# Attention operands of the first item copied by chunk, and its values moved between engines, in a two-layer transformer kernel

## The chip, the cores and the metric

The kernel runs on one core of one Trainium2 chip. The metric is the device time of one execution, in microseconds (us). Engines are named as in the profile: PE is TensorE, DVE is VectorE, ACT is ScalarE, POOL is GpSimd, SP is SyncE, whose queue issues the DMA transfers here.

## The reference

Two post-norm transformer layers over x of shape (2, 1024, 256), with 16 heads of 16. In layer 0 four heads share one group of keys and values:

```python
q = (x @ Wq + bq).reshape(B, T, 16, 16).transpose(0, 2, 1, 3)
k = (x @ Wk + bk).reshape(B, T, 4, 16).transpose(0, 2, 1, 3)
v = (x @ Wv + bv).reshape(B, T, 4, 16).transpose(0, 2, 1, 3)
k, v = jnp.repeat(k, 4, axis=1), jnp.repeat(v, 4, axis=1)
q_hat, k_hat = q / (norm(q) + EPS), k / (norm(k) + EPS)
scores = einsum(rope(q_hat * alpha * 4), rope(k_hat)) / 4      # causal
y = softmax(scores) @ v @ Wo + bo
x = layernorm(x + y)
x = layernorm(x + mxfp4(x) @ mxfp4(W).T + bias)                # layer 0's FFN
```

Layer 1 is an attention with 16 key heads (no normalisation of q and k), and a mixture of 8 experts, top 2, with a shared expert.

## The kernel before

**Tiling.** The 2048 tokens are 4 chunks of 512 (`NC`, `CH`). The kernel goes through a head (projections, rotation and lengths of layer 0's q and k, and its v), the attention of layer 0, a middle (layer 0's FFN and layer 1's projections), the attention of layer 1, and a tail with the experts. Every engine has one program, written out by hand in the order of the code; semaphores join them. An engine's instructions start in that order, so one that waits holds up all behind it.

**The head** (`head`) has 12 units `u`, three tiles for each chunk. For each unit: TensorE projects, DVE multiplies with the rotation tables (`turned`, L814), TensorE adds the rotated part, ACT keeps the result in a slot of `ops_mem` (`rot(u)`, `keep`, L742) and squares it; TensorE sums the squares and DVE turns them into factors per chunk (`factors`). TensorE transposes them (L689), ACT copies them (`keep_factors`, L763), TensorE spreads them over the rows (`spread_factors`, L699), DVE multiplies (`normalised`, L823). The product is split into three bf16 parts, high, middle and low: ACT casts the high part (`keep_hi`, L752), DVE subtracts it (`less_hi`, L830), ACT casts the middle part (`keep_mid`, L756), and GpSimd subtracts for the low part (L801), which counts in `s_parts[0]`. The values of the four chunks come from TensorE (L651); DVE adds the bias and writes them to `vres` (`values`, L833, L839). Those of chunks 2 and 3 stand in DVE's program between `less_hi(7)` and `less_hi(8)` (L901, L902).

**The attention** (`attention`, both layers) has 8 items, `NI`: 2 batches by 4 groups of 4 heads. Item `i` has two passes `c` of 512 queries over 12 steps `s` of 128 keys. TensorE makes scores (`scores`, L1238) into one of three pairs of PSUM banks, ACT takes the exponential (L1319), GpSimd masks the diagonal steps (L1335), TensorE multiplies with the values (`values_product`, L1255) into bank 6, two steps later. After each pass DVE copies bank 6 to `raw` (`take`, L1155), and `normalise` (L1157) transposes, inverts, transposes and multiplies into `yT` (L1162 to L1167). The first product of a pass waits until the take of the pass before is done (`s_taken`). DVE sets out the values of an item in `vstat` (L1149).

**Operands** (`Operands`). Scores contract over 99 rows: six combinations of parts by 16, and three rows for a shift. `stack(sp, i)` (L953) copies them from `parts_mem` to `qT` and `kT`, both in `ops_mem`, with two buffers `buf = i % 2`: 18 transfers in layer 0 and two more for the three rows (zeros on the q side, ones on the k side) for the first two items. In layer 1 there are 26. SP's order in each attention is: stack of item 0 once six units of parts are there (two chunks, batch 0), stack of item 1 once all parts are there, `no_shift` (L983), then the stacks of items 2 to 7:

```python
                ops.stack(sp, 0)
                sp.wait_ge(s_parts[layer], TILES[layer] * NC)
                ops.stack(sp, 1)
                ops.no_shift(sp)
                sp.wait_ge(ops.s_zero, 16 * GH)
```

`no_shift` fills `shiftT` with zeros in four transfers of three rows each. `shiftT` lies in `yT`, so DVE waits for them (`ops.s_zero`, L1186) after item 0's first take and ahead of its first `normalise`. From item 2 on a stack also waits for the scores of the item before last.

**The flag block** (`maxima`). Before each attention DVE and TensorE load a flag from memory and jump over a long block (`dve.If`, `pe.If`) that is only needed if scores could overflow; with these inputs it is jumped. In DVE's program the values of item 0 come behind that jump (`values(dve, 0)` in `attention`). TensorE's program behind it waits for free banks (`banks_free`, L912) and for item 0's stack (`ops.there(pe, 0)`), and makes the scores of the first two steps; then it waits for the values and makes those of the third.

**Where the buffers lie.** `ops_mem` columns 0 to 2047 and 4096 to 6143 are buffer 0 of `qT` and `kT`; the other halves are buffer 1. The kept tiles of units 0 to 5 lie in buffer 0, those of units 6 to 11 in buffer 1.

Of the kernel before, what the change touches and what calls it, by code (L numbers as in the profile page):

```python
# [17 lines left out]
T = 1024  # L18
# [50 lines left out]
def build(nc, a, out):  # L69
    ctx = ExitStack()  # L70
    with ctx:
# [506 lines left out]
        s_v, s_bo = sem("s_v1"), sem("s_bo")  # L578
        YN_COUNT, YN_HALF = 18, 11
# [13 lines left out]
        def head():  # L593
# [32 lines left out]
            def rot(u):  # L626

                b, j = u // (NU // 2), u % (NU // 2)
                o = 2048 * b + 512 * j if j < 4 else 4096 + 2048 * b + 512 * (j - 4)
                return ops_mem[:, o:o + 512]  # L630
# [174 lines left out]
            def _(dve):  # L805
# [95 lines left out]
                values(2)  # L901
                values(3)  # L902
# [9 lines left out]
            def banks_free(pe):  # L912

                pe.wait_ge(s_a_read, len(ORDER))
# [23 lines left out]
        class Operands:  # L938


            def __init__(self, layer):
# [3 lines left out]
                self.s_shifted = sem(f"s_shifted{layer}")  # L945
                self.s_zero, self.s_decided = sem(f"s_zero{layer}"), sem(f"s_decided{layer}")
                self.s_scores = sem(f"s_scores{layer}")

            def count(self, i):

                return 2 * NSLOT + (NSLOT if self.layer == 0 else 2 * NSLOT) + (2 if i < 2 else GH)

            def stack(self, sp, i):  # L953
# [20 lines left out]
                if i < 2:  # L974
                    sp.dma_start(qT[ROWS:KDIM, buf, :, :], a["zeros"][:, 0:GH * T].rearrange("r (h n) -> r h n", h=GH)
                                 ).then_inc(s, 16)
                    sp.dma_start(kT[ROWS:KDIM, buf, :, :], a["ones"].rearrange("r (h n) -> r h n", h=GH)
                                 ).then_inc(s, 16)
# [10 lines left out]
            def shift(self, dve, i):  # L989

                dve.wait_ge(self.s_stacked[i], 16 * self.count(i))
                for h in range(GH):
                    last = nc.vector.tensor_copy(qT[ROWS:KDIM, i, h, :], shiftT[32 * h:32 * h + 3, i, :])
                last.then_inc(self.s_shifted, 1)

# [122 lines left out]
        def attention(layer, ops, first, banks_free, buffer_free, gates=None, finish=None, ahead=None):  # L1118
            kh = KEYS_OF[layer]
            s_vstat = sem(f"s_vstat{layer}")  # L1120
# [14 lines left out]
            def _(sp):  # L1135
                buffer_free(sp)
                ops.stack(sp, 0)
# [8 lines left out]

            def values(dve, i):
                buf = i % 2
                nc.vector.tensor_copy(vstat[:, buf, :, 0:kh, HD * buf:HD * buf + HD],  # L1149
# [1077 lines left out]
```

## Time and profile before

| what | value |
|---|---|
| median of 3 runs | 809.42 us (808.75 to 810.59) |
| the profiled execution's own time | 807.32 us |
| its span | 805.6 us |
| TensorE busy | 728.9 us (90%) |
| DVE busy | 413.4 us (51%) |
| ACT busy | 394.9 us (49%) |
| GpSimd busy | 168.5 us (21%) |
| mean granted TensorE clock | 0.955 of full speed |

The profile is of one execution; its own time is 1.7 us over its span. A busy time says how long an engine had an instruction in it, and its share of the span is an average over parts of the kernel with different limits. The order of time gives, for each instruction, its start, its length and, in square brackets, how long its engine idled before it and what ended that; "issue" stands for an idle time that no event of the profile explains. An "x8" is a run of eight like instructions told as one line.

### The profile page before, as it was taken

To read this page: it belongs to the slowest core of one execution; us is meant where nothing else is said; L and a number is where in the kernel's file an instruction comes from. 1 tells how busy PE (TensorE), PEld (TensorE's weight loads), DVE (VectorE), ACT (ScalarE), POOL (GpSimd) and SP (SyncE) were. 2 spreads that over 40 slices of the span, in tenths; PEclk is the share of its full clock that TensorE was granted. 3 is DMA by queue.
4 is the path that set the end of the run, shared out by engine and by line. 5 is a ranking of instruction groups with operands and counts; after the bars stand their busy time and mean duration, and the time that the engine had idled before them with its cause. 6 is when DMAs were issued, how large, how long until landed. Compare 5 with 4: busy or idle time off the path is not lost.

```text
span 805.6 us, 10853 instructions
## 1 busy us (share of the span) xinstructions
PE 728.9 (90%) x3786; PEld 329.3 (41%) x3786; DVE 413.4 (51%) x998; ACT 394.9 (49%) x517; POOL 168.5 (21%) x185
## 2 busy tenths in 40 slices
PE   5998699999988867886999999989999999999996
PEld 1645222224322533442222222324466457448355
DVE  1578435334769798855043333365432842642524
ACT  1244688886877252543788888774121121130110
POOL 0012434443233132322133222331200200000000
PEclk9996599999999989879799999999999999999998
DMA  8401423332210000032444444470000000000000
GB/s 279 114 0 20 71 53 59 55 54 40 37 35 2 1 0 14 0 52 41 80 79 83 82 80 81 81 201 0 1 1 0 27 0 1 26 0 0 26 1 26
DMA packets 31602, 36.37 MB, mean 45 GB/s; under 512 B 7664, under 2 KB 19757, under 8 KB 31389
## 3 DMA queue, kind: packets, MB, share of 16 engines
q1 hardware_dynamic: 31541, 35.60, 21.8%
q8 instruction: 33, 0.54, 0.3%
q14 instruction: 28, 0.23, 0.1%
HBM read 12.74 MB, written 2.10 MB: 18 GB/s over the span
## 4 chain that ended last, share of the span: by engine, by line
PE 63%; DVE 15%; SPq 10%; ACT 5%; issue 4%; DMA 2%; POOL 0%; DVEq 0%; ACTq 0%; POOLq 0%
PE ps L1988 16%; PE ps L1255 12%; PE ps L1238 9%; PE ps L2012 9%; SPq L972 4%; SPq L965 4%; ACT probs L1319 3%; PE ps L1618 2%; PE ps L1605 2%; PE ps L398 2%; DVE stats L289 1%; PE ps L1632 1%; PE ps L643 1%; DVE raw L1155 1%; PE ps L1998 1%
## 5 line engine op out<-in xcount | busy, mean ns | idle before, releaser
L1319 ACT ACTIVATE probs<-ps 128x1024 f32<-128x1024 f32 (+1 forms) x320 | 276.0, 967 | 66.0 <-PE ps L1238 65.7
L1238 PE MATMUL ps<-ops_mem 99*128 99x512 bf16 (+3 forms) x768 | 164.0, 335 | 15.1 <-issue 5.5
L1255 PE MATMUL ps<-probs,vstat 128*32 128x512 f32 (+3 forms) x1536 | 166.1, 505 | 11.7 <-DVE raw L1155 7.4
L1988 PE MATMUL ps<-ops_mem,parts_mem 128*128 128x512 f32 x320 | 146.1, 602 | 1.2 <-DVE probs L2040 1.2
L1335 POOL TENSOR_SCALAR_AFFINE_SELECT probs<-probs 128x512 f32<-128x512 f32 x128 | 84.6, 661 | 225.3 <-ACT probs L1319 224.6
L1238 PEld LDWEIGHTS ps<-ops_mem 99*128 99x128 bf16 x768 | 57.6, 99 | 164.3 <-ACT probs L1319 87.9
L1155 DVE COPY raw<-ps 128x512 f32<-128x512 f32 x32 | 22.1, 691 | 140.8 <-PE ps L1255 140.6
L1934 ACT ACTIVATE ops_mem<-ps 128x512 f32<-128x512 f32 x40 | 23.9, 597 | 141.1 <-PE ps L1988 141.1
L1988 PEld LDWEIGHTS ps<-ops_mem,parts_mem 128*128 128x128 f32 x320 | 58.5, 190 | 67.8 <-issue 65.1
L2012 PE MATMUL ps<-parts_mem,probs 128*128 128x256 f32 x320 | 70.5, 380 | 0.0
L2012 PEld LDWEIGHTS ps<-parts_mem,probs 128*128 128x128 f32 x320 | 60.4, 190 | 8.3 <-issue 0.5
L1255 PEld LDWEIGHTS ps<-probs,vstat 128*32 128x32 f32 x1536 | 31.3, 108 | 73.9 <-issue 49.4
L2035 DVE TENSOR_TENSOR probs<-ops_mem,ps 128x512 f32<-128x512 f32 x40 | 27.5, 687 | 63.7 <-ACT ops_mem L1934 63.0
L1755 POOL TENSOR_TENSOR parts_mem<-probs,parts_mem 128x512 bf16<-128x512 f32 x16 | 22.0, 1387 | 68.3 <-ACT parts_mem L1725 68.3
L1162 DVE STREAM_TRANSPOSE den<-raw 128x512 f32<-128x512 f32 x32 | 22.7, 708 | 22.2 <-DMA yT<-in_zeros 21.5
L643 PE MATMUL ps<-yT,probs 128*128 128x512 f32 x48 | 27.2, 695 | 7.3 <-DMA yT<-in_xT 7.3
L1618 PE MATMUL ps<-ops_mem,w1qkv 128*128 128x512 f32 x64 | 30.9, 606 | 0.0
L744 ACT COPY ops_mem<-ps 128x512 f32<-128x512 f32 x12 | 7.0, 584 | 44.5 <-PE ps L667 44.5
L801 POOL TENSOR_TENSOR parts_mem<-parts_mem 128x512 bf16<-128x512 f32 x12 | 13.7, 1152 | 71.6 <-ACT parts_mem L756 71.5
L1167 DVE TENSOR_TENSOR yT<-raw,den 128x512 f32<-128x512 f32 x32 | 27.1, 848 | 1.1
L2040 DVE TENSOR_TENSOR probs<-probs,ps 128x512 f32<-128x512 f32 x32 | 22.0, 687 | 9.4 <-PE ps L1998 7.2
L1632 PE MATMUL ps<-probs,perm 128*128 128x512 f32 x32 | 21.9, 774 | 4.4 <-DVE probs L1784 4.4
(185 smaller groups left out, 720.8 us busy)
## 6 DMA issues: line engine op xcount, KB each, us to landing
ops_mem<-parts_mem SPq DMA_DIRECT2D x288, 64.0 KB
yT<-in_xT SPq DMA_DIRECT2D x4, 512.0 KB, 8.0
xres<-in_x SPq DMA_DIRECT2D x1, 2048.0 KB, 14.3
ops_mem<-parts_mem SPq DMA_DIRECT2D x48, 32.0 KB
out<-ops_mem SPq DMA_DIRECT2D x3, 512.0 KB, 3.0
rope<-in_rope SPq DMA_DIRECT2D x1, 1024.0 KB, 6.7
parts_mem<-in_wg SPq DMA_DIRECT2D x2, 512.0 KB, 5.9
parts_mem<-in_wu SPq DMA_DIRECT2D x2, 512.0 KB, 7.4
```

Source lines behind the costliest of these rows:

```text
L643: last = nc.tensor.matmul(ps[:, A + AT[m, n] % 2, :], w0qkv[:, kk, n * P:(n + 1) * P], xT0[:, kk, m * CH:(m + 1) * CH], start=kk == 0, sto ...
L965: sp.dma_start(qT[n * HD:n * HD + HD, buf, j::2, :], tq[32 * g + HD * j:32 * g + HD * j + HD, Q_PARTS[n], :, toks]).then_inc(s, 16)
L972: sp.dma_start(kT[n * HD:n * HD + HD, buf, j::2, :], tk[32 * g + HD * j:32 * g + HD * j + HD, K_PARTS[n], :, toks]).then_inc(s, 16)
L1155: nc.vector.tensor_copy(raw[:, :], ps[:, AV, :]).then_inc(s_taken, 1)
L1238: last = nc.tensor.matmul(ps[:, bank, o:o + CH - lo], kT[0:KDIM, buf, h if kh == GH else 0, kt * P:(kt + 1) * P], qT[0:KDIM, buf, h, c * C ...
L1255: last = nc.tensor.matmul(ps[32 * h:32 * h + 32, AV, lo:CH], vstat[:, i % 2, kt, h if kh == GH else 0, :], probs[:, s % PRING, h, 0:CH - l ...
L1319: nc.scalar.activation(o, banks, ACT.Exp, scale=score_scale).then_inc(s_exp, 1)
L1335: nc.gpsimd.affine_select(out=block_, in_=block_, compare_op=ALU.is_ge, fill=0.0, base=0, pattern=[[0, GH], [1, P]], channel_multiplier=-1 ...
L1618: last = nc.tensor.matmul(ps[:, A + n % 2, :], w1qkv[:, kk, n * P:(n + 1) * P], xT1[:, kk, :], start=kk == 0, stop=kk == 1)
L1632: nc.tensor.matmul(ps[:, R + u % 2, :], perm[:, :], u_sin[:, u % 2, :], start=False, stop=True).then_inc(s_rot, 1)
L1988: last = nc.tensor.matmul(ps[:, 4 + 2 * (e % 2) + m, :], w, xT[:, kk, :], start=kk == 0, stop=kk == 1)
L2012: last = nc.tensor.matmul(ps[:, t // 2, (t % 2) * C:(t % 2) * C + C], hT[:, e, t * P:(t + 1) * P], w, start=e == 0, stop=e == NE - 1)
```

## The change

It has five parts.

1. `rot(u)` uses eight slots in buffer 1 alone, in turn; from unit 8 on ACT waits for the product (`s_qn`) that frees the slot. Buffer 0 stays free.
2. Item 0's stack in layer 0 is `stack_first`: first the two transfers of zeros and ones, then chunk 0's 18 transfers when three low parts are written, then chunk 1's 18 when six are. The first 20 count in a new semaphore `s_early`, the others in the old one. TensorE waits for `s_early` before item 0's scores, and for the rest before step 4, the first of the second pass.
3. The values of item 0 are set out by DVE ahead of the flag block, in both layers (`first_values`); in layer 1 they wait for the values of two chunks instead of four.
4. The values of chunks 2 and 3 are copied from PSUM by ACT without the bias (`keep_values`), behind `keep_hi(7)` and `keep_hi(8)`.
5. GpSimd adds the bias to them in eight instructions, behind item 0's fourth mask; DVE waits for that before it sets out the values of item 4.

```diff
             def rot(u):
-                b, j = u // (NU // 2), u % (NU // 2)
-                o = 2048 * b + 512 * j if j < 4 else 4096 + 2048 * b + 512 * (j - 4)
+                j = u % 8
+                o = 2048 + 512 * j if j < 4 else 6144 + 512 * (j - 4)
                 return ops_mem[:, o:o + 512]
...
                 def keep(u):
                     act.wait_ge(s_rot, u + 1)
+                    if u >= 8:
+                        act.wait_ge(s_qn, u - 7)
...
+                def keep_values(m):
+                    act.wait_ge(s_a, AT[m, NTL] + 1)
+                    nc.scalar.copy(vres[:, NG:2 * NG, m % 2 * CT:(m % 2 + 1) * CT, 0:HD].rearrange("p g t d -> p t g d"),
+                                   ps[:, A + AT[m, NTL] % 2, 0:CT * 64].rearrange("p (t g d) -> p t g d", t=CT, g=NG)
+                                   ).then_inc(s_v0, 1)
...
                 keep_hi(7)
+                keep_values(2)
                 keep_mid(6)
                 keep_hi(8)
+                keep_values(3)
                 keep_factors(3)
...
                 less_hi(7)
-                values(2)
-                values(3)
                 less_hi(8)
...
-                pe.wait_ge(s_a_read, len(ORDER))
+                pe.wait_ge(s_a_read, len(ORDER) - 2)
+                pe.wait_ge(s_v0, 2)
...
+            def stack_first(self, sp):
+                s = self.s_stacked[0]
+                self.rows(sp, 0, self.s_early)
+                for m in range(2):
+                    toks = slice(m * CH, (m + 1) * CH)
+                    sp.wait_ge(s_parts[0], TILES[0] * (m + 1))
+                    for n in range(NSLOT):
+                        for j in range(2):
+                            sp.dma_start(qT[n * HD:n * HD + HD, 0, j::2, toks],
+                                         tq[HD * j:HD * j + HD, Q_PARTS[n], :, toks]
+                                         ).then_inc((self.s_early, s)[m], 16)
+                        sp.dma_start(kT[n * HD:n * HD + HD, 0, 0, toks], tk0[0:HD, K_PARTS[n], 0, toks]
+                                     ).then_inc((self.s_early, s)[m], 16)
...
-                ops.stack(sp, 0)
+                if layer == 0:
+                    ops.stack_first(sp)
+                else:
+                    ops.stack(sp, 0)
...
-                if layer == 1:
-                    dve.wait_ge(s_v, 2 * NC)
-                values(dve, 0)
...
-                ops.there(pe, 0)
+                if layer == 0:
+                    ops.early(pe)
+                else:
+                    ops.there(pe, 0)
...
                     for s in range(LAG, NS):
+                        if layer == 0 and i == 0 and s == 4:
+                            ops.there(pe, 0)
...
                         if layer == 0 and d == 3:
+                            if i == 0:
+                                pool.wait_ge(s_v0, 2)
+                                loaded(pool, "head")
+                                for t in range(TPB):
+                                    v = vres[:, NG:2 * NG, t, 0:HD]
+                                    last = nc.gpsimd.tensor_tensor(v, v, b_v[:, :].rearrange("p (g n) -> p g n", g=NG),
+                                                                   ALU.add)
+                                last.then_inc(s_v0, 1)
...
+        def first_values(layer):
+            @on("vector")
+            def _(dve):
+                if layer == 1:
+                    dve.wait_ge(s_v, NC)
+                values(dve, layer, 0)
+
+        first_values(0)
         maxima(0, ops[0])
...
+        first_values(1)
         maxima(1, ops[1])
```

## Rows read from the trace of the kernel before

**Rows 1.** The page: busy us (share of the span) x instructions.

```profile
PE 728.9 (90%) x3786; PEld 329.3 (41%) x3786; DVE 413.4 (51%) x998; ACT 394.9 (49%) x517; POOL 168.5 (21%) x185
```

**Rows 2.** Order of time, head: start us, us, engine, instruction [idle before].

```profile
62.06 1.15 POOL L801 TENSOR_TENSOR parts_mem<-parts_mem 128x512 bf16<-128x512 f32 x1 [2.94 <-ACT parts_mem L756]
...
83.30 1.14 DVE L839 TENSOR_TENSOR vres<-ps,b_v 128x64 f32<-128x64 f32 x8
...
83.31 0.58 ACT L763 COPY probs<-ps 60x512 bf16<-60x512 bf16 x1
...
84.95 1.29 DVE L823 TENSOR_TENSOR ps<-ps,ops_mem 128x512 f32<-128x512 f32 x2
...
87.71 3.46 POOL L801 TENSOR_TENSOR parts_mem<-parts_mem 128x512 bf16<-128x512 f32 x3 [0.80 <-ACT parts_mem L756]
```

**Rows 3.** The same view by engine, beginning of item 0 of layer 0.

```profile
82.25 0.63 PE L689 MATMUL ps<-identb,probs 128*60 128x128 bf16 x4 [0.47 <-DVE probs L870]
...
89.83 3.15 PE L1238 MATMUL ps<-ops_mem 99*128 99x512 bf16 x8 [4.07 <-DMA ops_mem<-in_ones]
...
90.94 3.35 ACT L1319 ACTIVATE probs<-ps 128x1024 f32<-128x1024 f32 x4 [1.36 <-PE ps L1238]
...
93.33 0.44 DVE L1149 COPY vstat<-vres 128x128 f32<-128x128 f32 x1 [4.39 <-issue]
```

**Rows 4.** The same view, the SP queue's issues.

```profile
74.83 1.44 SPq L965 DMA_DIRECT2D ops_mem<-parts_mem  x2
...
91.20 1.26 SPq L965 DMA_DIRECT2D ops_mem<-parts_mem  x2
...
103.57 3.14 SPq L986 DMA_DIRECT2D yT<-in_zeros  x4
```

**Rows 5.** The same view, end of item 0 and beginning of item 1.

```profile
112.79 0.71 DVE L1162 STREAM_TRANSPOSE den<-raw 128x512 f32<-128x512 f32 x1 [10.68 <-DMA yT<-in_zeros]
...
114.06 0.43 PE L1255 MATMUL ps<-probs,vstat 128*32 128x128 f32 x8
...
114.57 0.64 POOL L1335 TENSOR_SCALAR_AFFINE_SELECT probs<-probs 128x512 f32<-128x512 f32 x1 [2.03 <-ACT probs L1319]
...
114.58 1.17 DVE L1167 TENSOR_TENSOR yT<-raw,den 128x512 f32<-128x512 f32 x1
...
115.78 0.69 DVE L1155 COPY raw<-ps 128x512 f32<-128x512 f32 x1
...
116.62 1.06 PE L1255 MATMUL ps<-probs,vstat 128*32 128x512 f32 x8 [1.47 <-POOL probs L1335]
```

**Rows 6.** The same view, layer 1: the flag, first scores, item 1's first product.

```profile
378.93 0.14 DVE L1071 TENSOR_SCALAR flag<-guard 1x1 int32<-1x1 f32 x1
...
383.26 2.50 PE L1238 MATMUL ps<-ops_mem 99*128 99x512 bf16 x6 [5.18 <-issue]
...
409.83 1.06 PE L1255 MATMUL ps<-probs,vstat 128*32 128x512 f32 x8 [1.47 <-POOL probs L1335]
```

**Rows 7.** Groups by shape, ACT: xcount | busy us, mean ns | idle before.

```profile
L477 ACT ACTIVATE small<-small 128x32 f32<-128x32 f32 x4 | 0.9, 229 | 15.3 <-DVE small L495 15.3
```

**Rows 8.** The order of time, GpSimd's fifth mask and a later product of DVE.

```profile
108.42 0.63 POOL L1335 TENSOR_SCALAR_AFFINE_SELECT probs<-probs 128x512 f32<-128x512 f32 x1 [9.66 <-ACT probs L1319]
...
118.28 0.69 DVE L1167 TENSOR_TENSOR yT<-raw,den 128x512 f32<-128x512 f32 x1
```

**Rows 9.** TensorE after stalls; two stretches: us, busy (x), granted clock, DMA, GB/s.

```profile
229.31 1.07 PE L1255 MATMUL ps<-probs,vstat 128*32 128x512 f32 x8 [2.28 <-DVE raw L1155]
...
263.14 1.09 PE L1594 MATMUL ps<-ident,xres 128*128 128x128 f32 x8 [2.90 <-DVE raw L1155]
...
291.14 0.58 PE L1625 MATMUL ps<-none 1*128 1x512 bf16 x1 [5.29 <-DVE probs L1796]
...
265.00:269.00 4.00, 3.67 (x10) 0.57 0.01 4
...
291.00:298.00 7.00, 5.98 (x17) 0.65 0.00 0
```

More of the change, by code:

```diff
@@ L578, in build @@
         s_v, s_bo = sem("s_v1"), sem("s_bo")
+        s_v0 = sem("s_v0")
         YN_COUNT, YN_HALF = 18, 11
@@ L949, in count, with rows @@
             def count(self, i):
+                if self.layer == 0 and i == 0:
+                    return 3 * NSLOT
                 return 2 * NSLOT + (NSLOT if self.layer == 0 else 2 * NSLOT) + (2 if i < 2 else GH)
+            def stack_first(self, sp):
[11 more added lines that the diff above has]
+                                     ).then_inc((self.s_early, s)[m], 16)
+            def rows(self, sp, buf, s):
+                sp.dma_start(qT[ROWS:KDIM, buf, :, :], a["zeros"][:, 0:GH * T].rearrange("r (h n) -> r h n", h=GH)
+                             ).then_inc(s, 16)
+                sp.dma_start(kT[ROWS:KDIM, buf, :, :], a["ones"].rearrange("r (h n) -> r h n", h=GH)
+                             ).then_inc(s, 16)
             def stack(self, sp, i):
@@ L974, in stack @@
                 if i < 2:
[L975 to L978, printed above, removed]
+                    self.rows(sp, buf, s)
                 else:
@@ L991, in shift @@
                 dve.wait_ge(self.s_stacked[i], 16 * self.count(i))
+                if i == 0 and self.layer == 0:
+                    self.early(dve)
                 for h in range(GH):
@@ L994, in shift, with early @@
                 last.then_inc(self.s_shifted, 1)
+            def early(self, eng):
+                eng.wait_ge(self.s_early, 16 * (3 * NSLOT + 2))
             def there(self, pe, i):
@@ L1119, in attention @@
             kh = KEYS_OF[layer]
-            s_vstat = sem(f"s_vstat{layer}")
             s_scores = ops.s_scores
@@ L1145, in _ @@
                     ops.stack(sp, i)
-            def values(dve, i):
-                buf = i % 2
-                nc.vector.tensor_copy(vstat[:, buf, :, 0:kh, HD * buf:HD * buf + HD],
-                                      vres[:, i, :, 0:kh * HD].rearrange("p t (n d) -> p t n d", d=HD)
-                                      ).then_inc(s_vstat, 1)
             def take(dve, i, c):
@@ L1182, in _ @@
                     if i + 1 < NI:
-                        values(dve, i + 1)
+                        values(dve, layer, i + 1)
                     if i == 0:
@@ L1265, in _ @@
                 next(free)
-                ops.there(pe, 0)
+                if layer == 0:
+                    ops.early(pe)
+                else:
+                    ops.there(pe, 0)
                 scores(0, 0)
@@ L1271, in _ @@
                     more = i + 1 < NI
-                    pe.wait_ge(s_vstat, i + 1)
+                    pe.wait_ge(s_vstat[layer], i + 1)
                     for s in range(LAG, NS):
+                        if layer == 0 and i == 0 and s == 4:
+                            ops.there(pe, 0)
                         scores(i, s)
@@ L1327, in _ @@
                         pool.wait_ge(s_y, NI)
-                        pool.wait_ge(s_vstat, NI // 2)
+                        pool.wait_ge(s_vstat[layer], NI // 2)
                         for g in range(NG // 2):
@@ L1347, in _ @@
                                 pool.wait_ge(s_y, NI)
-                                pool.wait_ge(s_vstat, NI // 2)
+                                pool.wait_ge(s_vstat[layer], NI // 2)
                                 ahead.stage(pool, 0)
@@ L2095, in build, with values @@
         ops = [Operands(layer) for layer in range(2)]
+        s_vstat = [sem(f"s_vstat{layer}") for layer in range(2)]
+        def values(dve, layer, i):
+            buf, kh = i % 2, KEYS_OF[layer]
+            if i == NI // 2:
+                dve.wait_ge(*((s_v0, 3) if layer == 0 else (s_v, 2 * NC)))
+            nc.vector.tensor_copy(vstat[:, buf, :, 0:kh, HD * buf:HD * buf + HD],
+                                  vres[:, i, :, 0:kh * HD].rearrange("p t (n d) -> p t n d", d=HD)
+                                  ).then_inc(s_vstat[layer], 1)
+        def first_values(layer):
[5 more added lines that the diff above has]
+        first_values(0)
         maxima(0, ops[0])
```

1 line of the change is left out of this document (added).

## The prediction

> **What bounds the kernel now.** I read the page first, to see which engine the time hangs on. TensorE is busy nine tenths of the span [rows 1]. So a change pays only where it shortens a stretch in which TensorE stands idle, and only if nothing later in that stretch waits for something else.
>
> Next I read the order of time around the join of layer 0's head and its attention, as that is where the edits lie. Five things are to be seen there.
>
> First, how the head ends [rows 2]. DVE does its eight value adds (L839) from 83.30 to 84.44, between two subtractions; ACT copies the last factors at 83.31, TensorE spreads them, DVE multiplies at 84.95. From there the work is a strict relay of DVE and ACT to GpSimd's last three subtractions, which end at 87.71 + 3.46 = 91.17.
>
> Second, how item 0 begins [rows 3]. TensorE is idle from 85.76 to 89.83, until the ones of buffer 0 have landed. Its first two groups of scores end at 89.83 + 3.15 = 92.98, and the third stands behind the values, which DVE sets out from 93.33 to 93.77, after its flag. DVE's own way past the flag block costs it 4.39 us.
>
> Third, the SP queue [rows 4]. The first stack is issued from 74.83, when the sixth low part is written. The second starts at 91.20, 0.03 us after GpSimd's last subtraction, and its 20 transfers take SP to 103.57: 0.62 us each. Behind it come the four zero transfers, to 106.71.
>
> Fourth, **the wait that ends last at item 0's end** [rows 5]. After item 0's first take DVE idles 10.68 us for those zeros. From 112.79 it is one run of work: transpose, reciprocal, transpose, product, then the second take of `raw`, 115.78 to 116.47. TensorE had ended item 0's last product at 114.06 + 0.43 = 114.49 and item 1's third scores at 115.15; it idles 1.47 us to 116.62, when item 1's first product may overwrite the accumulator. The row names GpSimd, but the mask of that product was done at 115.21 and the take ended at 116.47: it is the take. Without the zeros it could have begun at about 114.5.
>
> Fifth, layer 1 has the same pattern: TensorE idles 1.47 us before item 1's first product at 409.83 [rows 6].
>
> **The change part by part.**
>
> *Operands by chunk, into a buffer kept free.* The ones and zeros rows go out long before, the first chunk's 18 transfers when three low parts are written (GpSimd's third ends at 62.06 + 1.15 = 63.21 [rows 2]) and the second chunk's 18 behind them. At 0.62 to 0.64 us each, the half-size ones taken like whole ones, that is 63.2 to 74.7 and then, as the sixth part is there at 74.80, to 86.4. SP issues 18 transfers more than before, and is still free 4.8 us before 91.2; only if each took over (91.2 - 63.2) / 36 = 0.78 us would the second stack slip. The eight-slot ring for the rotated tiles adds a wait of ACT on products that DVE finished several tiles earlier: nothing.
>
> TensorE's start is then no longer the DMA but its own way past the flag block. The trace doesn't show that alone. Its upper bound is the 4.07 us gap of before. In layer 1 it is 383.26 - 379.07 = 4.19 with the flag's load in it [rows 6]; in layer 0 that load fits into the 0.47 us before the factors' transposes at 82.25 [rows 3], so I take 3.7: start at 89.46 for 89.83, 0.37 earlier. The lower bound is near nothing (start at 85.8). The Trainium skill (Runtime: NRT & Kernel Launch, Instruction fetch mechanics) says that a taken branch to a page not yet fetched stops the engine for a fetch; Advanced Engine Details and Errata (Control Flow Timing) has about 108 ns for a compare and branch, by which TensorE would start some 3.9 us earlier. The 4.39 us on DVE and the 4.19 on TensorE speak for the first.
>
> *First values ahead of the flag.* The third scores then wait for two exponentials only. Four of those take 3.35 us from 90.94; two, from 0.37 earlier, end near 90.57 + 1.8 = 92.4. So the third scores start at 92.4 where they stood behind 93.77: **1.4 us earlier**. Bounds: 1.0 with no earlier start (two end at 92.8); 2.3 with an immediate one, as ACT is busy with the head's parts to 90.94 - 1.36 = 89.58 [rows 3]. So item 0 ends 1.0 to 2.3 us earlier. In layer 1 the copy now stands ahead of the flag's arithmetic: 0.43 us later there at most, covered by the 1.47 us that TensorE idles before 409.83; without that cover it would be a loss of 0.4.
>
> *Last values by ACT.* DVE is freed of 1.14 us of work between 83.30 and 84.35. ACT gains two copies of 128x256. No row is just that: 0.23 us for 32 columns [rows 7] and 0.58 for 512 [rows 2] bound it, and by a straight line it is 0.39. The second copy stands ahead of the last factors: 83.31 becomes about 83.70, the spread 84.3, done at 84.9. DVE was busy to 84.95 before and now is free at 84.2, so its product starts at 84.9 again. The two edits cancel: bounds -0.2 to +0.2 us on 91.17, for copies of 0.23 to 0.58. GpSimd's eight bias adds of 128x64 come after item 0's fourth mask; by 1.15 us for 512 columns [rows 2] each is about 0.15, by 1.15 at worst 9.2 in all, and GpSimd idles 9.66 us before its fifth mask at 108.42 [rows 8]: hidden. DVE's wait for them is at item 4.
>
> **The sum.** The 1.4 us is won ahead of item 0 and lost at its end. The zeros are behind the second stack, which is bound to 91.17, and that moves by 0 +- 0.2. So they land at 112.8 and TensorE goes on at 116.6; its idle stretch grows from 1.47 to 1.47 + 1.4 = 2.9 us. What is left is the product at 114.58, which took 1.17 us beside a mask of GpSimd and 0.69 without one [rows 5, 8]; the masks shift by 1.4, and I count half of the 0.48: -0.24. The profiled run is 807.32 (span 805.6), 2.1 under the median 809.42; the difference of -0.24 put on the median gives **809.2**.
>
> **Rivals.**
>
> *The clock falls in the longer stall (slower).* TensorE idled 2.28 us before 229.31 and kept its speed: eight products in 1.07 us, as the 1.06 at 409.83 [rows 6, 9]. After idling 5.29 us before 291.14 it ran at a lower granted clock, and also after 2.90 us before 263.14 [rows 9]. The new stall, 2.5 to 3.8 us, lies between. At half clock matmuls take up to twice as long. The granted clock was 0.57 over the 4 us from 265, a mixture of its levels 1 (2.4 GHz) and 0.5 (1.2 GHz): (1 - 0.57) / 0.5 x 4 = 3.4 us stood at half, which costs half of that, 1.7; after 291 it was 0.65 over 7 us, 4.9 us, with 2.4 as the most. That puts the time at 809.2 + 1.7 = 810.9, up to 811.6. It decides if the stall comes near those that lost the clock. The Trainium skill (TensorE: Matmul & The Clock Gate, HAM oscillation) warns of just this, the idle engine being put back to half rate; by its word the result would be that 810.9. Chance 0.20.
>
> *The start's gain comes through (faster).* If the zeros don't bind, or land sooner, item 1's first product starts one take (0.69) after item 0's last product, at about 114.5 - 1.4 + 0.8 = 113.9, 2.7 us earlier: 806.7, with bounds 805.8 and 807.1 from the bounds of 1.4. Against it stands the 10.68 us row [rows 5], and that the edits leave the zeros where they are in SP's order. Chance 0.15.
>
> *The head gets shorter.* If ACT's copies hide entirely, part of the 1.14 us reaches 91.17 and all behind it: 808.3 to 809. Chance 0.10.
>
> *It does not do what it says.* If the flag block takes the whole gap, TensorE starts at 89.83 as before; only 1.0 us moves, and is swallowed too: 809.4. Chance 0.10.
>
> **How the numbers follow.** My forecast has 0.42, and 0.03 is left for things unseen. No change within 0.2% (1.6 us, about what a measurement of this kernel can tell from no change) means 807.8 to 811.0: the forecast, the shorter head, the inactive change and half of the clock case, 0.42 + 0.10 + 0.10 + 0.10 = 0.72; I shade it to 0.66, as TensorE's start is poorly bounded on both sides, which gives faster 0.17 and slower 0.17. The range takes in most of both rivals: 806.6 to 811.5. The forecast's own range is 808.8 to 809.8.
>
> **What would show it.** Right: the first scores near 89.5, the third near 92.4; GpSimd's last subtraction at 91.2; zeros landed at 112.8; DVE's second take at 115.3 to 115.8; TensorE idle near 3 us before item 1's first product. The first branch cost is wrong if the first scores start before 88. The forecast is wrong if that product starts before 115.5, or if the granted clock is under 1 between 113 and 125. Layer 1 should stand at the same distances as before.

## The result, and the profile after

The changed kernel is slower. Its median is 813.92 us (810.08 to 817.5, 22 runs) where the kernel before, timed beside it, has 810.49 (806.99 to 816.41, 22 runs); the ratio is 1.0035 with a 95% interval of 1.002 to 1.005, which is 1.6 to 4 us. The profiled execution has a span of 811.0 us. I forecast 809.2, no change, with 806.6 to 811.5 as the range; on the kernel before's first median, 809.42, the ratio gives 812.3, above the range.

The profile of the kernel before is one of its fastest executions: 807.32 us where its median is 810.49. Its granted clock stands at 1.00 from 98 to 264 us and from 392 to 800 us, where the changed kernel's has 0.96 and 0.99. So the two profiles lie further apart than the medians, and the reading has to go place by place.

Four lines of the page: the span, the busy times, TensorE's granted clock in 40 slices, and the shares of the chain that ended last by engine.

```profile
span 811.0 us, 10879 instructions
...
PE 732.4 (90%) x3786; PEld 330.4 (41%) x3786; DVE 411.1 (51%) x990; ACT 395.5 (49%) x519; POOL 170.6 (21%) x193
...
PEclk9996689999989889899799999999999999999998
...
PE 61%; DVE 16%; SPq 11%; issue 4%; ACT 3%; DMA 3%; POOL 1%; DVEq 0%; ACTq 0%; POOLq 0%
```

TensorE is busy 3.5 us longer with the same 3786 matmuls [rows 1], so it did the same work more slowly. The order of time at the end of the head and the beginning of item 0 (start us, us, engine, instruction, [idle before]):

```profile
63.00 1.43 SPq L981 DMA_DIRECT2D ops_mem<-parts_mem  x2
...
82.85 0.38 ACT L766 COPY vres<-ps 128x256 f32<-128x256 f32 x1
...
84.40 1.30 DVE L837 TENSOR_TENSOR ps<-ps,ops_mem 128x512 f32<-128x512 f32 x2 [0.72 <-PE ps L701]
...
87.17 3.48 POOL L815 TENSOR_TENSOR parts_mem<-parts_mem 128x512 bf16<-128x512 f32 x3 [0.61 <-ACT parts_mem L761]
...
87.93 4.20 PE L1274 MATMUL ps<-ops_mem 99*128 99x512 bf16 x12 [2.72 <-issue]
...
88.31 0.22 DVE L2154 COPY vstat<-vres 128x128 f32<-128x128 f32 x1
...
89.04 4.26 ACT L1361 ACTIVATE probs<-ps 128x1024 f32<-128x1024 f32 x5
...
90.68 1.25 SPq L1006 DMA_DIRECT2D ops_mem<-parts_mem  x2
...
92.07 1.65 PE L1291 MATMUL ps<-probs,vstat 128*32 128x512 f32 x8
...
103.46 3.14 SPq L1024 DMA_DIRECT2D yT<-in_zeros  x4
```

Here nearly everything came as forecast. The head ran about half a microsecond early as a whole in this execution. Against that, DVE's multiplication at 84.40 stands where it stood before, ACT's copy takes 0.38 us (I took 0.39), and the second stack and the zeros start at 90.68 and 103.46 (91.20 and 103.57 in [rows 4]). But TensorE's first scores start at 87.93, with 2.72 us for the way past the flag block where I took 3.7 (2.5 to 3.1 in all nine profiles with operands copied by chunk), and ACT gets through its first five exponentials without a gap. Item 0's first product with the values starts at 92.07; in the kernel before it is this line, 2.7 us later:

```profile
94.79 1.94 PE L1255 MATMUL ps<-probs,vstat 128*32 128x512 f32 x8
```

The same view, end of item 0 and beginning of item 1, with item 1's first and second takes as the last lines:

```profile
110.54 0.43 PE L1291 MATMUL ps<-probs,vstat 128*32 128x128 f32 x8
...
112.63 0.71 DVE L1201 STREAM_TRANSPOSE den<-raw 128x512 f32<-128x512 f32 x1 [14.04 <-DMA yT<-in_zeros]
...
114.41 0.69 DVE L1206 TENSOR_TENSOR yT<-raw,den 128x512 f32<-128x512 f32 x1
...
115.14 0.69 DVE L1194 COPY raw<-ps 128x512 f32<-128x512 f32 x1
...
115.97 1.94 PE L1291 MATMUL ps<-probs,vstat 128*32 128x512 f32 x8 [4.35 <-DVE raw L1194]
...
123.26 0.69 DVE L1194 COPY raw<-ps 128x512 f32<-128x512 f32 x1 [4.93 <-PE ps L1291]
...
136.50 0.69 DVE L1194 COPY raw<-ps 128x512 f32<-128x512 f32 x1 [4.21 <-PE ps L1291]
```

Item 0's last product ends at 110.97, 3.5 us earlier than in [rows 5]. The zeros land at 112.63, as before, and DVE has waited 14.04 us for them instead of 10.68. DVE's product is down to 0.69 us. The take is at 115.14, TensorE's product at 115.97: 0.65 us earlier than before, after a stall of 4.35 us. And now eight products take 1.94 us instead of 1.06.

TensorE's busy time and clock by stretches of the changed kernel (stretch in us, length, busy and instructions, granted clock, DMA share, GB/s):

```profile
86.00:92.00 6.00, 4.02 (x12) 0.50 0.09 19
...
92.00:98.00 6.00, 6.00 (x47) 0.89 0.48 83
...
98.00:112.00 14.00, 13.42 (x100) 1.00 0.30 54
...
112.00:124.00 12.00, 7.88 (x47) 0.72 0.43 73
...
113.80:120.60 6.80, 4.63 (x22) 0.50 0.50 86
```

The same stretches of the kernel before, where they differ most:

```profile
92.00:98.00 6.00, 5.15 (x28) 0.51 0.49 85
...
112.00:124.00 12.00, 10.32 (x85) 1.00 0.40 69
```

Two things happened to the clock. It rose sooner (0.89 against 0.51 in the stretch from 92), which made item 0 shorter than I had reckoned and the stall longer. And it fell in the stall: 0.72 over the 12 us from 112, that is (1 - 0.72) / 0.5 x 12 = 6.7 us at 1.2 GHz, from 113.8 to 120.6. TensorE had 4.63 us of work in it; at full clock that would be half, 2.3 us less.

From here on I read one distance in every kernel: from item 0's second take to item 1's second take. In the kernel before it is 135.03 - 115.78 = 19.25, here 136.50 - 115.14 = 21.36. The line of the kernel before that [rows 5] doesn't hold:

```profile
135.03 0.69 DVE L1155 COPY raw<-ps 128x512 f32<-128x512 f32 x1 [4.21 <-PE ps L1255]
```

So the stall cost 2.11 us behind it; less the 0.64 us that the take was early, every take of the changed kernel up to item 6's first is 1.47 us later than in the kernel before. Behind that, this execution lost 2.7 us more at item 6 and 1.6 at the last item of layer 1, in two stalls of 2.29 and 1.74 us. Stalls of the same length stand in the kernel before, where the clock held in them; runs below show that it falls there in some executions with and without the change. Whether the change makes those falls more frequent isn't shown.

In layer 1 the copy that now stands ahead of the flag took 1.24 us, not the 0.43 that I had taken, while GpSimd was subtracting, and TensorE's first scores there come after 5.94 us of idleness instead of 5.18:

```profile
381.15 1.24 DVE L2154 COPY vstat<-vres 128x512 f32<-128x512 f32 x1
...
387.24 2.19 PE L1274 MATMUL ps<-ops_mem 99*128 99x512 bf16 x5 [5.94 <-issue]
```

### The profile page after: what moved, and what is told of

Same layout as the page of the kernel before. It is cut to its first block, busy times and chain, and to the rows that moved or that the text cites. A ratio compares the mean times of both kernels' runs of the same rounds, so it can differ in the third digit from the quotient of the medians.

```text
span 811.0 us, 10879 instructions
## 1 busy us (share of the span) xinstructions
PE 732.4 (90%) x3786; PEld 330.4 (41%) x3786; DVE 411.1 (51%) x990; ACT 395.5 (49%) x519; POOL 170.6 (21%) x193
## 4 chain that ended last, share of the span: by engine, by line
PE 61%; DVE 16%; SPq 11%; issue 4%; ACT 3%; DMA 3%; POOL 1%; DVEq 0%; ACTq 0%; POOLq 0%
PE ps L2039 16%; PE ps L1291 11%; PE ps L2063 9%; PE ps L1274 8%; SPq L1006 5%; SPq L1013 4%; PE ps L1669 2%; PE ps L1656 2%; PE ps L398 2%; DMA yT<-in_zeros 2%; ACT probs L1361 2%; DVE stats L289 2%; DVE raw L1194 1%; PE ps L645 1%; PE ps L669 1%
## 5 line engine op out<-in xcount | busy, mean ns | idle before, releaser
L1291 PE MATMUL ps<-probs,vstat 128*32 128x512 f32 (+3 forms) x1536 | 168.8, 512 | 14.9 <-DVE raw L1194 11.9
L1274 PE MATMUL ps<-ops_mem 99*128 99x512 bf16 (+3 forms) x768 | 165.9, 338 | 14.3 <-issue 9.5
L645 PE MATMUL ps<-yT,probs 128*128 128x512 f32 x48 | 25.3, 651 | 7.2 <-DMA yT<-in_xT 7.2
L1669 PE MATMUL ps<-ops_mem,w1qkv 128*128 128x512 f32 x64 | 30.9, 605 | 0.0
L1683 PE MATMUL ps<-probs,perm 128*128 128x512 f32 x32 | 20.2, 717 | 4.4 <-DVE probs L1835 4.4
```

What stands on the lines that cost most here:

```text
L645: last = nc.tensor.matmul(ps[:, A + AT[m, n] % 2, :], w0qkv[:, kk, n * P:(n + 1) * P], xT0[:, kk, m * CH:(m + 1) * CH], start=kk == 0, sto ...
L1274: last = nc.tensor.matmul(ps[:, bank, o:o + CH - lo], kT[0:KDIM, buf, h if kh == GH else 0, kt * P:(kt + 1) * P], qT[0:KDIM, buf, h, c * C ...
L1291: last = nc.tensor.matmul(ps[32 * h:32 * h + 32, AV, lo:CH], vstat[:, i % 2, kt, h if kh == GH else 0, :], probs[:, s % PRING, h, 0:CH - l ...
L1669: last = nc.tensor.matmul(ps[:, A + n % 2, :], w1qkv[:, kk, n * P:(n + 1) * P], xT1[:, kk, :], start=kk == 0, stop=kk == 1)
```

## The experiments

**Theory 1**: the gain ahead of item 0 is lost at the zeros, and the stall that takes its place costs TensorE its clock. **Theory 2**, in one form or another: the loss comes from the other edits (ACT's copies, GpSimd's adds, 18 more transfers, layer 1's copy), or from the length of the stall alone. Twelve kernels test them. Each was timed in five rounds against the kernel before; ratios are against that, with 95% intervals. Each has one profile. "The distance" is that between the two takes above.

### The zeros in SP's gap

```diff
+                if layer == 0:
+                    banks_free.mem_free(sp)
+                    ops.no_shift(sp)
                 sp.wait_ge(s_parts[layer], TILES[layer] * NC)
                 ops.stack(sp, 1)
-                ops.no_shift(sp)
+                if layer == 1:
+                    ops.no_shift(sp)
```

`mem_free`, whose definition is left out here, has SP wait until TensorE has made the head's last projection and its last sum of squares, so that the head is done with `yT`.

On the changed kernel:

> The changed kernel, with the four zero transfers of layer 0 issued between the first item's last copies and the second stack, in the gap in which SP stands idle (about 87.5 to 90.7 us). Theory 1 (the gain ahead of item 0 is lost at the zeros, and TensorE's clock falls in the stall there): the zeros land by 97, no stall of over 0.5 us before item 1's first product, which starts at 111.5 to 113 for 115.97; the granted clock stays 1.0 from 112 to 125; the time is 4 to 7 us under the kernel before, ratio 0.991 to 0.995. Theory 2 (the loss comes from the other edits: ACT's copies, GpSimd's adds, more transfers, the copy ahead of layer 1's flag): that product starts earlier, but no more than 2 us of it is left at the end of layer 0, and the ratio stays at 0.999 or over.

Measured: ratio 0.9961 (0.9937 to 0.9985), median 806.74. Its order of time, SP's zeros, DVE's work after item 0, and TensorE's first product of item 1:

```profile
87.51 3.15 SPq L1029 DMA_DIRECT2D yT<-in_zeros  x4
...
98.58 0.69 DVE L1203 COPY raw<-ps 128x512 f32<-128x512 f32 x1 [9.69 <-PE ps L1300]
...
99.37 0.71 DVE L1210 STREAM_TRANSPOSE den<-raw 128x512 f32<-128x512 f32 x1
...
111.91 0.69 DVE L1203 COPY raw<-ps 128x512 f32<-128x512 f32 x1 [10.06 <-PE ps L1300]
...
112.75 1.07 PE L1300 MATMUL ps<-probs,vstat 128*32 128x512 f32 x8 [0.31 <-DVE raw L1203]
```

The zeros were there when DVE wanted them (its transpose follows the first take at once), the stall is 0.31 us, the product starts at 112.75, and the distance of the takes is 19.25 again. All takes up to the end of layer 0 are 3.87 us earlier than before. By the ratio the kernel is 3.2 us (1.2 to 5.1) faster than the one before, with all the other edits in place. That speaks against Theory 2's first form, and it is less than the 4 to 7 us that I expected: in this profile the last take of layer 1 is only 1.48 us early, and the clock fell once near 538 and once near 562 us, where it had held in the profile of the kernel before.

On the kernel before:

> The kernel before with the same move of the zeros alone. Theory 1: the stall of 1.47 us shrinks to 0.3, the product starts at 115.4 for 116.62, ratio 0.998 to 0.999; so the change is worth 3 to 4 us once the zeros are out of the way. Theory 2: the same 1.2 us here, but the changed kernel with the zeros moved is no faster than this one.

Measured: the stall shrank to 0.31 us and the distance from item 0's first take to its second from 14.50 to 13.33 us, the expected 1.2. The ratio, 1.0017 (0.9992 to 1.0042) for 0.998 to 0.999 expected, doesn't show it; in its profile the clock fell at item 6's stall. So the time alone leaves the 1.2 us unproven. But it answers Theory 2: of the two kernels with the zeros moved, timed side by side, the changed one has 806.74 against 810.63, so the change is worth 3.9 us once the zeros are out of the way (3 to 4 expected).

### The stall filled with work

```diff
                         scores(i, s)
+                        if layer == 0 and i == 1 and s == LAG:
+                            for _ in range(16):
+                                nc.tensor.matmul(ps[:, 7, :], kT[0:KDIM, 1, 0, 0:P], qT[0:KDIM, 1, 0, 0:CH],
+                                                 start=True, stop=True)
                         values_product(i, s - LAG)
```

> The changed kernel with 16 matmuls of 128x512 more, whose result nobody reads, in front of item 1's first product, so that TensorE has work in the stall. Nothing else is moved. Theory 1: the product starts at 115.9 to 116.2 as in the changed kernel, but the granted clock stays 1.0 until 125 and the next take of DVE comes at 121.2 to 121.6 for 123.26 (1.5 to 2.1 us earlier); ratio 0.999 to 1.001. Theory 2: the take stays within 0.5 us of 123.26 or the ratio stays at 1.003.

Measured: ratio 0.9979 (0.9957 to 1.0001), median 807.58. Order of time:

```profile
111.67 3.62 PE L1319 MATMUL ps<-ops_mem 99*128 99x512 bf16 x16
...
114.93 0.69 DVE L1194 COPY raw<-ps 128x512 f32<-128x512 f32 x1
...
115.77 1.06 PE L1291 MATMUL ps<-probs,vstat 128*32 128x512 f32 x8 [0.48 <-DVE raw L1194]
...
120.95 0.69 DVE L1194 COPY raw<-ps 128x512 f32<-128x512 f32 x1 [2.82 <-PE ps L1291]
...
134.18 0.69 DVE L1194 COPY raw<-ps 128x512 f32<-128x512 f32 x1 [4.21 <-PE ps L1291]
```

and the stretch from 112 to 124, with its granted clock:

```profile
112.00:124.00 12.00, 11.37 (x78) 1.00 0.43 73
```

Sixteen matmuls whose result nobody reads make the changed kernel faster; the interval lies wholly under its own, 1.002 to 1.005. The product starts at 115.77, nearly as without them, the clock stays at 1.00, the distance of the takes is 19.25, and the next take came at 120.95 (123.26 - 120.95 = 2.31 us sooner, for 2.11 + the 0.20 by which the product starts earlier). This is the strongest evidence for Theory 1: nothing about the waits is changed, only what TensorE does during one. The take came a little earlier and the ratio lower than expected (121.2 to 121.6; 0.999 to 1.001). Between the middles of the two ratios lie 4.5 us, twice what the takes show; the other half has no place in these profiles that I can name.

### The stall lengthened in the kernel before

```diff
                         dve.wait_ge(ops.s_zero, 16 * GH)
+                        if layer == 0:
+                            dve.wait_ge(s_taken, 1)
+                            for n in range(4):
+                                nc.vector.transpose(den[:, :], raw[:, :]).then_inc(s_delay, 1)
+                                dve.wait_ge(s_delay, n + 1)
```

> The kernel before with four more transposes of DVE (0.71 us each, into a buffer that is written again at once) after the zeros' wait, which lengthens the stall before item 1's first product from 1.47 to about 4.4 us and changes nothing else. Theory 1: the product starts 2.9 to 3.0 us later, at 119.6, the clock falls to 0.5 behind it, and the next take is 4.4 to 5.2 us later than 121.79; ratio 1.0055 to 1.0065. Theory 2 (a stall costs its own length): the next take is 2.9 to 3.1 us later, ratio 1.0035 to 1.004.

```profile
118.24 1.94 PE L1261 MATMUL ps<-probs,vstat 128*32 128x512 f32 x8 [3.79 <-DVE raw L1156]
```

and its stretch:

```profile
112.00:124.00 12.00, 8.14 (x61) 0.86 0.48 82
```

Measured: from item 0's first take to its second 16.82 us for 14.50, and the distance of the takes 138.07 - 117.40 = 20.67 for 19.25. So the kernel before gets the same disease from a longer stall alone: 2.3 us for the delay (the stall is 3.79 us, not 4.4) and 1.4 for the clock. The next take itself came at 124.87, 3.08 us behind 121.79. By the letter that is Theory 2's forecast of 2.9 to 3.1; but this execution was 0.70 us early at item 0's first take, and from there the next take is 3.78 us later, which a delay of 2.3 us alone doesn't give. The ratio is 1.0091 (1.0062 to 1.0121), 5 to 10 us, more than both: in its profile the clock also fell at item 1's stall of layer 1, which was 2.36 us long. The direction is shown, the size in the time was under-expected.

### Parts of the change undone

The first values of layer 0 behind the flag again:

```diff
-        first_values(0)
         maxima(0, ops[0])
+        first_values(0)
```

> The changed kernel with layer 0's first values behind the flag again, as in the kernel before. Theory 1 (the stall before item 1's first product is as long as the start of item 0 is early): the third group of scores waits for the values, near 92.7 for 91.3, item 0 ends about 1.5 us later than in the changed kernel, the stall is 2.5 to 3.3 us for 4.35; the product starts at 115.9 to 116.1 all the same. The clock may fall or not; if it does the next take is at 123.0 to 123.4, if not at 121 to 121.3. Theory 2 (the early values themselves cost): the next take is at 121.8 or earlier with the clock fallen.

```profile
91.90 1.03 PE L1274 MATMUL ps<-ops_mem 99*128 99x256 bf16 x4 [0.89 <-DVE vstat L2154]
...
115.84 1.06 PE L1291 MATMUL ps<-probs,vstat 128*32 128x512 f32 x8 [1.83 <-DVE raw L1194]
```

Its stretches from 112 and from 226:

```profile
112.00:124.00 12.00, 9.96 (x83) 1.00 0.43 74
...
226.00:238.00 12.00, 9.71 (x46) 0.72 0.10 19
```

Measured: ratio 0.9999 (0.9974 to 1.0024). The third scores wait for the values (0.89 us), the clock rises later (0.50 from 92 to 98, for 0.89), the stall is 1.83 us, shorter than the 2.5 to 3.3 that I expected, and the clock held: distance 19.25. At item 6 it fell.

Item 0's operands copied as before:

```diff
-                if layer == 0:
-                    ops.stack_first(sp)
-                else:
-                    ops.stack(sp, 0)
+                ops.stack(sp, 0)
...
```

The waits of TensorE and DVE for the early transfers are taken out with it.

> The changed kernel with item 0's operands copied as in the kernel before, all 20 transfers once six low parts are there. Theory 1: the first scores start at 89.4 to 89.9 instead of 87.93, the third near 91.5 to 92.3, the stall before item 1's first product is 3.0 to 4.0 us and the product itself stays at 115.9 to 116.2; with a fallen clock the next take is at 123.0 to 123.5. So undoing this part alone leaves most of the loss: ratio 1.001 to 1.004. Theory 2 (the 18 transfers more are the cost): ratio under 1.000.

```profile
93.16 3.15 PE L1266 MATMUL ps<-ops_mem 99*128 99x512 bf16 x8 [5.94 <-DMA ops_mem<-in_ones]
...
118.26 1.56 PE L1283 MATMUL ps<-probs,vstat 128*32 128x512 f32 x8 [1.57 <-POOL probs L1363]
```

Its stretch from 112:

```profile
112.00:124.00 12.00, 10.37 (x79) 0.86 0.34 59
```

Measured: ratio 1.001 (0.9984 to 1.0036). In this execution the head and the stack came late, so item 0 began at 93.16 and the stall was 1.57 us, not 3 to 4. Yet the clock fell at it, and the distance is 20.78. With the run above it shows that of two stalls of 1.57 and 1.83 us the shorter lost the clock and the longer kept it: length alone does not decide. Neither part alone shows a loss by its ratio, but both intervals reach into the changed kernel's 1.002 to 1.005.

Layer 1's first values behind the flag:

```diff
-        first_values(1)
         maxima(1, ops[1])
+        first_values(1)
```

> The changed kernel with layer 1's first values behind the flag, as in the kernel before. In the three kernels with the copy ahead of the flag TensorE's idle time before layer 1's first scores is 5.94, 6.25 and 6.67 us, in the three with it behind 5.18, 5.14 and 5.43. Theory 1 (that 0.8 to 1.5 us is covered, since item 0's second take waits for the zeros): the idle time is back at 5.1 to 5.5, the second take of layer 1 stands at the same 29.9 to 31.1 us behind the first transfer of layer 1's second stack, ratio as the changed kernel's, 1.002 to 1.005. Theory 2 (it is the part of the loss that the first stall doesn't explain): ratio 1.001 to 1.003, about 1 us under the changed kernel's.

Measured: ratio 1.0027 (1.0003 to 1.0051), distance of the takes in layer 0 21.48 after a stall of 4.21 us. TensorE's idle time before layer 1's first scores was 5.88 us, not 5.1 to 5.5. Over all profiles it is 5.1 to 5.9 with the copy behind the flag (five, mean 5.5) and 5.9 to 6.7 with it ahead (nine, mean 6.3). So the copy costs about 0.8 us there, where I had reckoned 0.43 at most. That is swallowed too: item 0's second take of layer 1, which waits for zeros as in layer 0, stands 30.9 to 32.8 us behind the last matmul ahead of the flag with the copy behind it, and 30.4 to 32.0 with it ahead. The ratio fits both theories' forecasts; the median, 813.86, is the changed kernel's 813.92. Taking the copy back doesn't take the loss back.

### The other stalls

```diff
+                        if layer == 0 and i == 6 and s == 6:
+                            pe.wait_ge(ahead.s_half_sum, 4)
+                            idle_work(0, 8)
+                        if layer == 1 and i == 1 and s == LAG:
+                            idle_work(1, 5)
+                        if layer == 1 and i == 7 and s == 6:
+                            pe.wait_ge(first.s_half_sum, 2)
+                            idle_work(1, 6)
```

`idle_work(buf, n)`, whose definition is left out here, issues n of the matmuls of the first filling into bank 7, on operand buffer buf. First the kernel with the zeros moved and the eight matmuls at item 6 alone:

> The changed kernel with the zeros in SP's gap, and with 8 matmuls more in front of item 6's second pass in layer 0, where TensorE stalls for 2.29 us in every kernel so far; the clock fell behind that stall in two of six profiles (the changed kernel's and that of the kernel before with the zeros moved). Theory 1 (clock falls at short stalls are luck of each execution, and account for the spread of the times): the clock stays 1.0 from 222 to 240 and the item is no longer than in the kernel before; the median is 0 to 1.5 us under that of the changed kernel with the zeros moved, ratio 0.993 to 0.997. Theory 2 (the spread has another source): median and spread as without the 8 matmuls, or 2 us worse for the added work.

Measured: ratio 0.9931 (0.9903 to 0.996), the clock at 1.00 through item 6, median 805.79 against 806.74. In the nine profiles without those eight matmuls the clock fell at that stall of 2.28 or 2.29 us in four, one of them of the kernel before with the zeros moved. But the spread of the runs, which Theory 1 also put down to such falls, stayed: 8.3 us for 8.8.

Then all three, on the changed kernel, on the changed kernel with the first stall filled too, and on the kernel before:

> The changed kernel with matmuls that nobody reads in the three other stalls of the two attentions: 8 before item 6's second pass of layer 0, 5 before item 1's first product and 6 before item 7's second pass of layer 1. The stall that the change lengthened is left as it is. So the luck of the later stalls is taken out and the first stall's price is left. Theory 1 (that stall alone makes the change slower, by the clock): the clock falls behind it (next take 1.3 to 2.1 us later against the kernel before) and at none of the three; 2 to 3 us slower than the kernel with this stall filled too. Theory 2 (there is a further loss of 1 us or more elsewhere in the change): it stays when both are filled.

> The same with 16 matmuls in the stall before item 1's first product as well. Theory 1: no fallen clock from 95 to 258 and in layer 1's attention behind its first scores; the next take 0.5 to 0.9 us earlier than in the kernel before; median 0.5 to 1.0 us under the kernel before with the same three stalls filled. Theory 2: it is 1 us or more over that one.

> The kernel before with the same three stalls filled: the base for the other two. Theory 1: 0 to 2 us under the kernel before, since the clock fell at none of the three in its first profile but in about half of the others' at item 6. The changed kernel with the three filled is 1.4 to 2.1 us over this one, ratio 1.0017 to 1.0026. Theory 2: it is 3 us or more over it.

The stretches of the changed kernel with the three filled, from 112, 226 and 538:

```profile
112.00:124.00 12.00, 7.97 (x49) 0.72 0.39 67
...
226.00:238.00 12.00, 11.29 (x75) 1.00 0.25 45
...
538.00:550.00 12.00, 11.10 (x79) 1.00 0.43 134
```

and with the first stall filled as well:

```profile
112.00:124.00 12.00, 11.19 (x77) 1.00 0.40 68
...
226.00:238.00 12.00, 11.29 (x77) 1.00 0.14 26
...
538.00:550.00 12.00, 11.55 (x83) 1.00 0.03 8
```

| kernel | median us | lowest to highest | ratio | distance of the takes |
|---|---|---|---|---|
| changed, three stalls filled | 810.1 | 807.15 to 812.36 | 0.9973 (0.9952 to 0.9993) | 21.48 |
| changed, all four filled | 806.48 | 805.62 to 807.12 | 0.9939 (0.9918 to 0.996) | 19.24 |
| before, three filled | 809.2 | 804.97 to 810.9 | 0.9969 (0.9951 to 0.9988) | 19.25 |

Of these four stalls the clock falls at the first alone when the three are filled (0.72, 1.00, 1.00). It also fell twice elsewhere, at about 430 and 566 us, in the profiles of both kernels with the three filled (0.79 over the 8 us from 426 and from 564) and at neither place in the profile with all four (1.00). Filling the first stall too takes 3.6 us off the median (expected 2 to 3); a part of that can be the luck of those two places. It leaves a spread of 1.5 us in six runs, where the others of the table have 5.2 and 5.9 in twelve. The changed kernel is 0.9 us by the medians over the kernel before with the same three filled, and 0.0004 by the ratios, whose intervals nearly coincide; I expected 1.4 to 2.1. It is 2.7 us under it with all four, where I expected 0.5 to 1.0. Both lie on the side of a base that is itself slowed: the kernel before keeps its own stall of 1.47 us at item 1, and a stall of 1.57 lost the clock above. No profile of it caught that, so it stays an inference. Theory 2's remainder, a further loss of 1 us or more that no filling removes, is not there.

At last the zeros moved, with the three filled:

> The changed kernel with the zeros issued in SP's gap and the same three stalls filled: the fastest that these findings give. Theory 1: 5 to 7 us under the kernel before, ratio 0.991 to 0.994, take of item 1's first pass 3.5 to 4.2 us earlier. Theory 2: no better than the changed kernel with the zeros moved alone, 0.9961.

Measured: 804.79 (802.36 to 806.83), ratio 0.9922 (0.9897 to 0.9948), item 1's first take 4.4 us earlier than before. It is 6.3 us faster than the kernel before, in the 5 to 7 expected. Its six runs still spread over 4.5 us, and its clock fell once more, near 423 us, at a stall of 2.12 us that was not filled.

## Why the prediction was wrong

**The sum's parts.** The head's balance (0 +- 0.2), ACT's copy (0.39 against 0.38), the 18 transfers more, GpSimd's adds (2.26 us in all, behind item 0's fourth mask) and the zeros' landing (112.8 against 112.63) were right. So was the central step: the gain at item 0's start is swallowed by the zeros. Layer 1's copy costs 0.8 us and not 0.43, but is covered, as I had said. The -0.24 for DVE's product was right in kind; it got the whole 0.48.

**The size of the stall.** "Its idle stretch grows from 1.47 to 1.47 + 1.4 = 2.9 us" was the mis-sized term: 4.35. Item 0's last product ended 3.5 us earlier, not 1.4. Its first product was already 2.7 us earlier: about 0.5 of that is the head, early as a whole in this execution while the zeros landed only 0.16 sooner, and about 0.8 comes from the way past the flag block, 2.72 us for the 3.7 I took. The test that I gave for that (scores before 88) came out against me by 0.07 us; the early head helped it, but 3.7 was too much in all nine profiles. The last 0.8 us I had not reckoned at all: with no gap between the second and the third scores the clock rose sooner (at 93.3 to 96.4 us in the eight profiles with a gap of at most 0.2 us, at 97.3 to 98.2 in the six with a longer one or with late scores), and TensorE ran item 0 faster. The bounds of 1.0 to 2.3 held no term for the clock.

**The choice of the case.** This is the step that failed: the sum put the cost of the longer stall at nothing behind it, and the runs show 2.11 us of lost clock. I named the mechanism that decides, with its place, and gave it 0.20, because I took the stall to lie between rows that kept the clock and rows that lost it. Even the 2.9 us that I expected was as long as the 2.90 us in [rows 9] that had lost it (with a second idle time of 1.10 us close behind), and 4.35 us was longer still; all four stalls of 3.8 us or more before item 1's first product lost the clock. I should have asked what the clock does in every stretch that the change moves, and not only where I expected a stall. The price, 1.7 with 2.4 as the most, was sound: 2.11 behind a stall of 4.35, 2.23 twice, 1.42 in the delayed kernel. Net of the 0.64 that is 1.47 us in the profiles. That the whole time of this rival, 810.9 up to 811.6, still lies under 812.3 is the open part below.

**What stays open.** Those 1.47 us lie just below the measured 1.6 to 4; the rest of the ratio's middle, some 1.3 us, no single profile shows as the change's. With three later stalls filled in both kernels the change costs 0.9 us by the medians, and the ratios don't tell that from nothing. So the mechanism at the first stall is settled, and filling it takes the whole loss away (0.9979 for 1.0035); but how much of the mean loss arises there, and how much in the luck of the later stalls, is not. ACT's copies and GpSimd's adds were never undone by themselves; what speaks for them costing nothing is that the kernel with the zeros moved is faster with both in place.

**The rivals.** The faster one failed as I argued, since the zeros bind; moving them in SP's order gave more than it had priced (3.9 us in the takes for 2.7; that the median, 806.74, is the rival's 806.7 is chance). The shorter head and the inactive change didn't come about. The Trainium skill (TensorE: Matmul & The Clock Gate, HAM oscillation) describes the case that happened: a wait between two stretches of matmuls puts the engine back to half rate, and the next stretch starts slow. The granted clock of 0.50 from 113.8 to 120.6 us agrees with it.

## What to carry to other kernels

When a start is moved earlier, follow the gain to the next wait that does not move. If it is swallowed there, it has become a longer stall of TensorE, and that stall has a price of its own: the clock behind it. Ask where the swallowing wait's release is issued, for four small transfers moved ahead in their queue turned the change from a loss into a gain of 3.9 us, while the same move in the kernel before changed nothing that its time could tell; and if a wait can't be moved, spare matmuls in it can cost less than nothing.

## What the runs showed of the hardware

- TensorE's granted clock fell in single executions after stalls as short as 1.57 us and held after 1.83 and 2.29: the same stall of item 6 kept it in five profiles of nine and lost it in four. The four stalls of 3.79 to 4.35 us before item 1's first product all lost it. Where the takes show the price of a fall, it is 1.4 to 2.8 us.
- The time of a run goes with its clock: of the changed kernel's 22 runs, the fastest (810.08 us) has a mean granted clock of 0.951 and the slowest two (817.22 and 817.5) 0.941 and 0.943. With four stalls filled the lowest and the highest of six runs were 1.5 us apart, and the mean granted clock in the profile was 0.957 for 0.949. That these four stalls make the spread isn't shown: filling one left 8.3 us, filling three 5.2 and 5.9.
- A copy of DVE of 128x512 that takes 0.42 us later in the same profile took 1.24 us in each of the nine profiles where it ran beside two subtractions of GpSimd. That these are the cause wasn't tested.
